# A decoder layer on one core: experts' rows from two factors, quantised tiles in pairs, maxima beside the norm's root

## What is computed

```python
x = x + attention(layernorm(x))                    # 16 heads, low-rank q and kv, rotary part
x = x + quantised_expert(layernorm(x), fside, ctx) # per batch
x = x + top2_of_8_experts(layernorm(x))            # silu(x w1) * (x w3) w2, weighted

def smooth_quant_linear(x, w):        # x [512, D], w [O, D]
    s = sqrt(max|x| per column / max|w| per column)
    xs, ws = x / s, w * s
    x_scale, w_scale = row maxima of |xs|, |ws|, each / 127
    return (round(xs / x_scale) @ round(ws / w_scale).T) * x_scale * w_scale.T

def quantised_expert(x, fside, ctx):
    gate, up = split(smooth_quant_linear(x, fside))
    return smooth_quant_linear(silu(gate) * up, ctx)
```

## Time and profile before

| | |
|---|---|
| median of 3 runs | 1187.24 us (1186.02 to 1187.73) |
| profiled execution | 1186.23 us, its span 1184.4 us |
| busy in the span | PE 990.1 (84%), DVE 968.2 (82%), ACT 670.5 (57%), POOL 291.5 (25%) |
| attention with its preparation | to about 868 us |
| last projections beside the first norm | 868 to 897 us |
| quantised layers | 897 to 1057 us |
| experts | 1057 to 1184.4 us |

### The profile page before, as it was taken

How to read it: one execution, slowest core, us unless ns; L and a number is a source line. 1 busy time by engine, 2 the same in 40 slices (tenths; PEclk the granted TensorE clock), 3 DMA queues, 4 the chain that set the end, 5 groups by cost and what they waited for, 6 DMA issues and landing times.

```text
span 1184.4 us, 18766 instructions
## 1 busy us (share of the span) xinstructions
PE 990.1 (84%) x6124; PEld 574.9 (49%) x6124; DVE 968.2 (82%) x2685; ACT 670.5 (57%) x1465; POOL 291.5 (25%) x508
## 2 busy tenths in 40 slices
PE   0456667999999999999999999999887565659997
PEld 0234444555555555555555555555445353435553
DVE  5757749989989888989989988888857888758886
ACT  1446557676666666667666666665504765743331
POOL 1036523232232222223223222221110222221110
PEclk9768679999999999999999999999988788769999
DMA  9300004333333336433325343345357130002323
GB/s 348 135 1 1 1 14 70 74 72 59 70 65 63 69 62 131 73 56 70 71 58 137 63 68 59 68 96 104 74 186 202 48 107 1 0 1 44 82 72 89
DMA packets 217328, 90.77 MB, mean 77 GB/s; under 512 B 191497, under 2 KB 202761, under 8 KB 216721
## 3 DMA queue, kind: packets, MB, share of 16 engines
q1 hardware_dynamic: 217232, 89.58, 32.7%
HBM read 36.06 MB, written 7.34 MB: 37 GB/s over the span
## 4 chain that ended last, share of the span: by engine, by line
PE 51%; DVE 31%; ACT 7%; issue 5%; POOL 3%; DMA 3%; SPq 0%; DVEq 0%; POOLq 0%; ACTq 0%
PE bank L1914 12%; PE bank L1864 8%; PE bank L1899 6%; PE bank L1812 3%; PE bank L1843 3%; DVE arena L774 3%; DVE arena L687 2%; PE bank L1882 2%; DVE arena L689 2%; PE bank L1886 2%; PE bank L1884 2%; PE bank L1885 2%; PE bank L1883 2%; DVE arena L1515 2%; DVE arena L1522 1%
## 5 line engine op out<-in xcount | busy, mean ns | idle before, releaser
L1204 ACT ACTIVATE arena<-bank,arena,scal 128x128 f32<-128x128 f32 (+3 forms) x256 | 157.7, 616 | 112.3 <-POOL arena L1045 111.2
L1914 PE MATMUL bank<-arena 128*128 128x512 f16 x768 | 179.2, 381 | 1.9 <-DVE arena L1548 1.9
L1522 DVE SCALAR_TENSOR_TENSOR arena<-arena 128x128 f16<-128x128 f32 (+3 forms) x256 | 142.2, 555 | 9.1
L1864 PE MATMUL bank<-arena 128*128 128x512 f16 x576 | 137.6, 385 | 0.0
L1045 POOL TENSOR_TENSOR arena<-arena,scal 128x1 f32<-128x1 f32 x256 | 51.2, 201 | 347.5 <-DVE arena L1498 345.8
L1515 DVE TENSOR_SCALAR arena<-arena 128x128 f16<-128x128 f32 (+3 forms) x256 | 125.4, 490 | 7.4 <-DVE arena L1507 0.8
L1498 DVE TENSOR_REDUCE arena<-bank 128x1 f32<-128x128 f32 (+3 forms) x256 | 123.7, 483 | 7.8 <-PE bank L1887 6.7
L1899 PE MATMUL bank<-arena 128*128 128x512 f16 (+3 forms) x768 | 117.6, 304 | 11.2 <-DMA arena<-arena 6.0
L1914 PEld LDWEIGHTS bank<-arena 128*128 128x128 f16 x768 | 73.1, 98 | 81.1 <-issue 4.7
L1899 PEld LDWEIGHTS bank<-arena 128*128 128x128 f16 x768 | 71.8, 99 | 62.7 <-issue 16.1
L1223 ACT ACTIVATE arena<-bank 32x512 f32<-32x512 f32 x128 | 75.2, 587 | 26.1 <-PE bank L1843 24.8
(11 more groups left out here) (200 smaller groups left out, 2053.5 us busy)
## 6 DMA issues: line engine op xcount, KB each, us to landing
arena<-in_L_attn_w_qb SPq DMA_DIRECT2D x1, 4608.0 KB, 21.6
arena<-arena SPq DMA_TRANSPOSE x272, 2.8
arena<-in_x SPq DMA_DIRECT2D x4, 1024.0 KB, 6.9
arena<-in_L_attn_w_o SPq DMA_DIRECT2D x1, 4096.0 KB, 31.9
arena<-in_fside_BxS2xS SPq DMA_DIRECT2D x4, 1024.0 KB, 7.3
arena<-in_L_ffn_w SPq DMA_DIRECT2D x8, 512.0 KB, 7.5
out<-arena SPq DMA_DIRECT2D x16, 256.0 KB, 2.3
arena<-in_x SPq DMA_DIRECT2D x12, 256.0 KB, 2.9
```

Of the source, the lines that this page charges most:

```text
L1204: act.activation(pf(k), banks[S_BANKS[G % 3]][:, 0:n], ACT.Exp, bias=NB[:, k:k + 1], scale=sc_exp, accum_out=SUM[:, k:k + 1]).then_inc(s_e ...
L1522: dve.scalar_tensor_tensor(out=ph_part(k, 1), in0=pf(k).rearrange("p (t c) -> p t c", c=P), scalar=R4[:, k:k + 1], in1=ph_part(k, 0), op0= ...
L1864: last = pe.matmul(banks[Q_BANK][:, :], wq(a, c, (i & 7) * 2 + h), ct(bp, b, c, 0, L), start=(k == 0), stop=(k == 3 * QC - 1))
L1914: last = pe.matmul(banks[Y_BANK][:, :], ot(gp, a, k, (q & 3) * P, P), wo(b, gp * GH + k), start=(k == 0 and n == 0), stop=(k == GH - 1 and ...
```

## The change

Three edits:

1. In the experts, GpSimd makes a second column, minus mean times inverse root (`mnr`), and ScalarE makes the normalised rows as x times the root plus that column. VectorE's `apply` goes. ScalarE's `apply(n + 2)` stands behind `front(n + 1)` and ahead of `silus(n + 1)`. Three waits keep the columns from being overwritten.
2. Two rounded tiles are transposed into the two halves of one bank, and ScalarE copies both with one instruction. TensorE waits for no copy within a matrix; the matrix's pair k waits for the rows' pair k.
3. `norm_batch` is cut in two. In the second round `norm_rows` stands inside `scales`, behind the four reductions of the matrix; in the first round it stays directly behind `norm_batch`.

```diff
@@ -328,7 +328,8 @@
         MH = take(E * FF, bf16)
         MHT = [take(E * FF, bf16) for _ in range(2)]
         ms = take(100)
-        m6, mmv, mcar, meps, mrs = ms[:, 0:6], ms[:, 6:8], ms[:, 8:9], ms[:, 9:10], ms[:, 10:11]
+        m6, mmv, mcar, meps, mrs, mnr = (
+            ms[:, 0:6], ms[:, 6:8], ms[:, 8:9], ms[:, 9:10], ms[:, 10:11], ms[:, 11:12])
         SCO, MX, IXF, IOTA, WV, WV2 = (ms[:, 16 + 8 * k:24 + 8 * k] for k in range(6))
         IX = ms[:, 64:72].bitcast(u32)
         DZ, EZ, DEN, P1, P2, mcar2 = (ms[:, 72 + k:73 + k] for k in range(6))
@@ -490,7 +491,11 @@
 
             def rstd_of(n):
                 pool.wait_ge(m_var, n + 1)
+                if n > 0:
+                    pool.wait_ge(m_norm, n)
                 pool.tensor_tensor(mrs, meps, half[:, 0:1], ALU.pow).then_inc(m_rstd, 1)
+                pool.wait_ge(m_rstd, 2 * n + 1)
+                pool.tensor_scalar(mnr, mmv[:, 0:1], mrs, -1.0, ALU.mult, ALU.mult).then_inc(m_rstd, 1)
 
             def second(n):
 
@@ -544,10 +549,10 @@
                 wid, li = LIN[l][0], layer_of(r, l, u)
                 c = wid // P
                 tr, te, dst = ((x_t, x_te, QXT), (w_t, w_te, QWT))[kind]
-                for t in range(TB):
-                    act.wait_ge(tr, li * TB + t + 1)
-                    act.activation(dst[u].rearrange("p (c q) -> p c q", c=DC)[:, 0:c, t * P:(t + 1) * P],
-                                   bankb[4 * u + t % 2][:, 0:wid].rearrange("p (c q) -> p c q", c=c),
+                for k in range(2):
+                    act.wait_ge(tr, li * TB + 2 * k + 2)
+                    act.activation(dst[u].rearrange("p (c t q) -> p t c q", c=DC, t=TB)[:, 2 * k:2 * k + 2, 0:c],
+                                   bankb[4 * u + k].rearrange("p (t c q) -> p t c q", t=2, c=DC)[:, :, 0:c],
                                    ACT.Copy).then_inc(te, 1)
 
             def output_scales(r, l, u):
@@ -579,6 +584,12 @@
             act.wait_ge(w2_in, 16)
             act.activation(W2B, W1S, ACT.Copy).then_inc(w_cast, 1)
 
+            def apply(n):
+                act.wait_ge(m_rstd, 2 * n + 2)
+                if n > 0:
+                    act.wait_ge(m_t, n)
+                act.activation(MXT, xall(n), ACT.Identity, bias=mnr, scale=mrs).then_inc(m_norm, 1)
+
             def front(n):
                 act.wait_ge(m_t, n + 1)
                 act.activation(XTB, banks[0][:, :], ACT.Copy).then_inc(m_tb, 1)
@@ -592,12 +603,17 @@
                     last = act.activation(MSG[n % 2][:, k * 512:(k + 1) * 512], banks[2 + k][:, :], ACT.Silu)
                 last.then_inc(m_silu, 1)
 
+            apply(0)
             front(0)
+            apply(1)
             silus(0)
             front(1)
+            apply(2)
             for n in range(1, NT - 1):
                 silus(n)
                 front(n + 1)
+                if n + 2 < NT:
+                    apply(n + 2)
             silus(NT - 1)
 
         def later_dve(dve, tail):
@@ -634,6 +650,10 @@
                 dve.wait_ge(q_agg, s + 1)
                 dve.tensor_scalar(qeps, qmv.rearrange("p (t a) -> p t a", a=2)[:, :, 1], 1e-5, None, ALU.add)\
                     .then_inc(q_var, 1)
+
+            def norm_rows(r, u):
+
+                s = r * 2 + u
                 dve.wait_ge(q_rstd, s + 1)
                 for t in range(TB):
                     dve.tensor_scalar(NX[u][:, t * D:(t + 1) * D], xall(batch_of(r, u) * TB + t),
@@ -648,6 +668,8 @@
                 link = chain(c_own, li, 4)
                 am = AM[u]
                 for t in range(2 * TB):
+                    if t == TB and l == 0 and r > 0:
+                        norm_rows(r, u)
                     a = (TB + t if t < TB else t - TB) * 4
                     dve.wait_ge(c_t, li * 2 * TB + t + 1)
                     dve.tensor_reduce(AMT[u][:, a:a + c], banks[4 * u + t % 4][:, 0:wid].rearrange("p (c q) -> p c q", c=c),
@@ -704,7 +726,7 @@
                     X = XB[batch_of(r, u)]
                     dve.tensor_tensor(X, X, HF[u], ALU.add).then_inc(x2_made, 1)
 
-            tail(norm_stats, norm_batch, scales, quantise)
+            tail(norm_stats, norm_batch, norm_rows, scales, quantise)
             for h in HALVES:
                 r, l, u = h
                 prev = preceding(h)
@@ -729,19 +751,14 @@
                 dve.bn_stats(m6, xall(n)).then_inc(m_stat, 1)
                 dve.wait_ge(m_stat, n + 1)
                 dve.memset(mcar, 0.0)
+                if n > 0:
+                    dve.wait_ge(m_rstd, 2 * n)
                 dve.bn_aggr(mmv, m6).then_inc(m_agg, 1)
                 dve.wait_ge(m_agg, n + 1)
                 dve.tensor_scalar(meps, mmv[:, 1:2], 1e-5, None, ALU.add).then_inc(m_var, 1)
 
-            def apply(n):
-                dve.wait_ge(m_rstd, n + 1)
-                if not (n == 0):
-                    dve.wait_ge(m_t, n)
-                dve.tensor_scalar(MXT, xall(n), mmv[:, 0:1], mrs, ALU.subtract, ALU.mult).then_inc(m_norm, 1)
-
             def norm(n):
                 stats(n)
-                apply(n)
 
             def route(n):
 
@@ -793,7 +810,6 @@
                 gate(n)
                 stats(n + 2)
                 add_out(n - 1)
-                apply(n + 2)
                 route(n + 1)
             gate(NT - 2)
             add_out(NT - 3)
@@ -832,15 +848,13 @@
 
             def quantised_t(r, l, u, kind):
                 wid, li = LIN[l][0], layer_of(r, l, u)
-                made, done, te = ((qx_r, x_t, x_te), (qw_r, w_t, w_te))[kind]
+                made, done = ((qx_r, x_t), (qw_r, w_t))[kind]
                 for t in range(TB):
                     pe.wait_ge(made, li * TB + t + 1)
-                    if t >= 2:
-                        pe.wait_ge(te, li * TB + t - 1)
-                    elif kind == 1:
-                        pe.wait_ge(x_te, li * TB + TB)
+                    if kind == 1 and t % 2 == 0:
+                        pe.wait_ge(x_te, li * 2 + t // 2 + 1)
                     for q in range(wid // P):
-                        last = pe.transpose(bankb[4 * u + t % 2][:, q * P:(q + 1) * P],
+                        last = pe.transpose(bankb[4 * u + t // 2][:, t % 2 * D + q * P:t % 2 * D + (q + 1) * P],
                                             rounded_rows(l, u, kind)[:, t * D + q * P:t * D + (q + 1) * P], identb[:, :])
                     last.then_inc(done, 1)
 
@@ -854,7 +868,7 @@
 
             def layer(r, l, u):
                 c, li = LIN[l][0] // P, layer_of(r, l, u)
-                pe.wait_ge(w_te, li * TB + TB)
+                pe.wait_ge(w_te, li * 2 + 2)
                 for t in range(TB):
                     if t == 3:
                         pe.wait_ge(wsb_made, li + 1)
@@ -1740,17 +1754,19 @@
             out_lo(2 * NPAIR - 2)
             out_lo(2 * NPAIR - 1)
 
-            def tail(norm_stats, norm_batch, scales, quantise):
+            def tail(norm_stats, norm_batch, norm_rows, scales, quantise):
                 add_y(NPAIR - 5)
                 norm_stats(0, 0, 0)
                 norm_stats(0, 0, 1)
                 norm_batch(0, 0)
+                norm_rows(0, 0)
                 add_y(NPAIR - 4)
                 scales(0, 0, 0)
                 add_y(NPAIR - 3)
                 norm_stats(0, 1, 0)
                 norm_stats(0, 1, 1)
                 norm_batch(0, 1)
+                norm_rows(0, 1)
                 add_y(NPAIR - 2)
                 quantise(0, 0, 0, 0)
                 add_y(NPAIR - 1)
```

## The result

| | before | after |
|---|---|---|
| median | 1186.63 us (4 runs, 1184.40 to 1187.73) | 1169.85 us (4 runs, 1168.90 to 1171.18) |
| ratio | | 0.9862, 95% interval 0.9843 to 0.9880 |
| profiled execution, its span | 1186.23 us, 1184.4 us | 1171.18 us, 1169.4 us |

The medians differ by 16.8 us, the spans of the two profiled executions by 15.0; the profiled execution of after is the slowest of its four. "Product" is the first quantising product of a half layer's rows (L687 before, L709 after; in the first half layer that of the matrix), `stats(0)` the first statistics of the experts.

The account below looks back on a forecast made before the run. VectorE was taken as the chain in the quantised layers and experts' loop. Gains 3.7 + 2.2 + 1.2 + 1.9 + 7.5 = 16.5 us gave 1170.7 us; own range 1167 to 1173, high end 1176 with rivals.

Parts of the forecast that it names:

- (a): Quantised layers: the wait moves to ScalarE and half of the 9.0 us is lost; 1175.2 us; chance 0.10.
- (e): Whole change: bank halves still held back, rows come no earlier; within 2 us of before; chance 0.03.
- Rows on ScalarE: Experts' loop: VectorE loses `apply`, 0.61 us a block, period 7.06 to 6.45; 7.9 over 13 blocks, 7.5 net.
- (b): Experts' loop: ScalarE's queue sets the period at 6.75 us; 1174.6 us; chance 0.08.
- (c): Experts' loop: TensorE, held by the turned rows, sets the period at 6.67 us; 1173.5 us; chance 0.06.
- (b2): Experts' loop: ScalarE's dearer pass lengthens the period, 7.06 + 0.23 us; 1181.2 us; chance 0.02.
- (d): Experts' loop: ScalarE changes its function table twice in every block; slower, 1199 us; chance 0.03.
- The start: Start of the experts' loop: the longer way through GpSimd and ScalarE costs about 0.4 us, once.
- The pairs: Quantised layers: TensorE no longer held by copies; 3.7 us in the first half layer, 2.2 and 1.2 elsewhere.
- Edges: Before each of four second-kind half layers: VectorE's wait for TensorE shrinks by 0.54 us each, 2.2 together.
- the last half layer: End of the quantised layers: TensorE's 2.43 us wait for a copy goes; 1.2 us, between 0 and 2.43.
- The maxima: Second round's norm, two places: four matrix reductions cover the wait for GpSimd's root; 0.95 us each, 1.9.

Follow-up runs that it names:

- the large copy: Changed kernel plus an unused ScalarE copy of 864 columns directly behind each `apply` in the experts' loop: 1174.68 us, ratio 0.9898.
- a shorter sum: Changed kernel with the experts' residual sum made for 128 of 512 columns only: 1169.47 us, ratio 0.9854.
- edit 1 alone: Kernel before with only the experts' normalised rows moved to ScalarE, quantised layers as before: 1180.84 us, ratio 0.9960.
- the reversed one: Changed kernel with ScalarE's order turned in the experts' loop, `silus(n)` ahead of `apply(n+1)`: 1176.06 us, ratio 0.9912.
- edit 3 alone: Kernel before with only the matrix's maxima put ahead of the normalised rows in the second round: 1182.02 us, ratio 0.9963.
- four copies: Changed kernel, two tiles to a bank and TensorE free, but each tile copied by its own instruction, four instead of two per matrix: 1170.04 us, ratio 0.9855.
- edit 2 alone: Kernel before with only the quantised tiles put two to a bank and copied in pairs: 1178.31 us, ratio 0.9932.
- TensorE's order: Changed kernel with the next half layer's row transposes and `spread` ahead of the transposes back, before second-kind layers: 1167.31 us, ratio 0.9840.

## Why the prediction was right, point by point

**Bound and mechanism.** Right in both stages: the gain came where VectorE waited or worked, and the waits went that the sum had named. Each edit alone moves its own stretches by what it moves in the whole change. With that, (a) and (e) fell: of the 9.0 us for the quantised layers nothing was lost to ScalarE, 10.0 came.

**Rows on ScalarE**, predicted 7.9 for the loop: 7.69. The step of 0.61 was 0.61 in the twelve undisturbed blocks (7.06 to 6.45); in the mean it is 0.592 (7.057 to 6.465), for the one block of 6.65. The way through ScalarE was forecast to end 6.1 after the gate and ended at 5.98 (1079.87 less 1073.89): the product took 0.27 where I took 0.2, the pass 0.81 instead of 0.78, but the two silus 1.06 instead of 1.19, since they overlap. So 0.47 spare instead of 0.35, and rival (b) fell by measurement; a longer ScalarE is what brings it about (6.828 with the large copy). (Its own steps, 6.1 and six times 0.1, make 6.70 and not the 6.75 that it was priced with.) Rival (c) was near: 6.42 was forecast for TensorE, and that is what the gates that wait for it show with a shorter sum. The power behind GpSimd's product was not held in the steady blocks: it waits 0.16 for VectorE.

Rival (b2), a period of 7.29, fell as well: edit 1 alone has 6.499. The pass is dearer on ScalarE, 0.81 against 0.55, but it lies in time that ScalarE had to spare. The rule of the Trainium skill against the change, additions and products on VectorE ("ScalarE: Activation LUTs", Rules for kernel authors), has the direction of that price right and doesn't decide the period here. Rival (d) fell too: the last table load stands at 865.0 us. That agrees with the Trainium skill, which puts identity into every set ("ScalarE: Activation LUTs", Table sets).

**The start** cost 0.66 instead of 0.4. The step counted the longer way of one block's rows; the first gate waits 2.85 us for silus queued behind `apply(1)` as well. That this order is the price is shown by the reversed one, where the start takes 19.21 us.

**The end of the loop** was not in the sum, and gives back 2.08 us. From `gate(14)` to the end (after; the window over the last `down`, then in order of time):

```profile
1162.49:1165.03 2.54, 2.54 (x8) 0.77 (x8) 0.00 (x0) 0.00 (x0) 0.00 (x0) 0.72 0.28 108
```

```profile
1157.21 2.16 DVE L791 SCALAR_TENSOR_TENSOR arena<-bank,arena 128x128 bf16<-128x128 f32 x8 [0.49 <-PE bank L933]
...
1162.49 2.54 PE L942 MATMUL bank<-arena 128*128 128x512 bf16 x8 [3.65 <-DMA arena<-arena]
...
1165.08 0.69 DVE L798 TENSOR_TENSOR arena<-bank,arena 128x512 f32<-128x512 f32 x1 [5.11 <-PE bank L942]
```

Before, in the same views:

```profile
1179.29:1181.19 1.90, 1.90 (x8) 0.69 (x8) 0.00 (x0) 0.00 (x0) 0.00 (x0) 1.00 0.37 142
```

```profile
1174.00 2.16 DVE L774 SCALAR_TENSOR_TENSOR arena<-bank,arena 128x128 bf16<-128x128 f32 x8 [0.20 <-DMA arena<-arena]
...
1179.29 1.90 PE L928 MATMUL bank<-arena 128*128 128x512 bf16 x8 [3.50 <-DMA arena<-arena]
1181.22 0.69 DVE L781 TENSOR_TENSOR arena<-bank,arena 128x512 f32<-128x512 f32 x1 [4.46 <-PE bank L928]
```

The last gate comes 5.72 after `gate(14)`, before 5.43: with VectorE's step shortened, `up` is late, 0.29. The last `down` has a granted clock of 0.72 instead of 1.00, so a part of it runs at 1.2 GHz, after 3.65 us idle instead of 3.50, and takes 2.54 instead of 1.90: 0.66 to the last sum. From that sum to the end it is 4.32 instead of 3.18, 1.14. That is the last store, which lands 3.2 us after its issue instead of 2.0. In the view of the DMA, after and then before (queue: packets, MB, share; issue: count, KB, us to landing):

```profile
q8 instruction: 1, 0.02, 2.4%
...
out<-arena SPq DMA_DIRECT2D x1, 256.0 KB, 3.2
```

```profile
out<-arena SPq DMA_DIRECT2D x1, 256.0 KB, 2.0
```

While the store is under way, the queue that the profile calls instruction moves one packet of 16 KB. Only one other kernel has that, the one with ScalarE's order turned, and its last store takes 2.7; in the ten without it takes 2.0. The slow turns of the hidden rows go with the same queue: of the 192 turns in the twelve traces, the 154 with no such packet between issue and landing took 3.04 to 3.12 us, the 6 with one of 8 KB 3.44 to 3.49, and the 32 with one of 16 KB 3.03 to 4.86, 27 of them 3.4 or more. The last such turn of edit 1 alone, and then the one ahead of it:

```profile
q8 instruction: 1, 0.02, 1.4%
...
arena<-arena SPq DMA_TRANSPOSE x1, 4.6
```

```profile
arena<-arena SPq DMA_TRANSPOSE x1, 3.1
```

The kernels without edit 1 end in 15.83 to 16.33, those with it in 17.6 to 19.6. In five of the latter the last gate waits for such a slow turn (4.5 to 4.9 us), in four for `up`, and it comes 5.7 to 7.2 after `gate(14)`. Their last `down` takes 2.3 to 3.6; but in the kernels with edit 2 or edit 3 alone it takes 2.4 as well, so the fall of the clock is not of edit 1 alone. Of the 2.08 us only the 0.29 of the late gate is shown to follow from the edit. Why a packet meets just that turn in five of the nine kernels with the edit and in none of the other three, and why the clock falls, are open.

**The pairs**, 7.1 predicted, 7.48 measured. First half layer 3.82 against 3.7: the 0.1 for ScalarE's rounding was not lost, since GpSimd's root of the ratios lasts longer (to 909.26 us, the rounding to 908.99). Edges 2.14 against 2.2, but 0.37 to 0.82 apiece. The hole itself behaved as the step says, 0.57 to 0.59 at each for the 0.54 taken. At 6 to 7, the edge of the earlier trace rows, VectorE's wait for the `spread` shrinks as well, from 1.05 to 0.80, which is the upper bound's case. At 2 to 3 and 3 to 4 the four reductions behind the hole take 0.19 and 0.18 longer. That the sum came out is partly luck, and so is the last half layer, 1.52 where the middle of 0 to 2.43 was taken. The 0.16 a pair that ScalarE gains, noted beside TensorE's freedom and not in the sum, are worth nothing that shows, as four copies tell.

**The maxima**: mis-sized, 1.9 against 2.55, and above the bound of 1.15 each. Two steps failed. The last tile was not late: the row transposes took 2.03 us for four tiles, the faster pace. And the bracket of 1.13 understates what the wait cost: from the variance's last instruction to the next it was 1.31 (987.32 to 988.63), now 0.08 (981.40 to 981.48), so 1.23, since the instruction that isn't held starts before the one ahead has ended. Before:

```profile
987.32 0.17 DVE L635 TENSOR_SCALAR arena<-arena 128x4 f32<-128x4 f32 x1
```

**The sum.** By spans 15.0 was gained of 16.5: quantised layers 1.0 better, loop and start 0.5 worse, end 2.1 worse. By medians it was 16.8. The 1.8 between the two is no gain: the profiled execution of before lies 0.4 below the median of its four runs, that of after 1.3 above. The forecast of 1170.7 is 0.9 above the median and 0.5 below the profiled execution. That is closer than its terms: the errors cancel, and that they do is luck. The low end, called the sum of the better ends, took the edges and the last half layer at their middle; with their upper bounds of 3.4 and 2.43 that sum is 19.8 and not 17.4.

## What to carry to other kernels

Price a removed wait from start to start of the engine's instructions, not by the idle time in the bracket, and take it where the next engine's queue stands: the gain of two tiles a bank was that TensorE's queue ran past the copies, not that there were fewer of them. An operation can go to a slower engine if that engine's way from release to use ends ahead of its reader; count it in order of time, and then ask which engine is next (here TensorE, 0.03 us behind, with GpSimd's queue close by). Count the first and the last block of a loop by themselves, and look at the same stretch in kernels without the edit before you put its loss down to it.

## What the runs showed of the hardware that I had not expected

- A `spread` of 16 fp32 matmuls takes 2.05 us in after, at a granted clock of 1.00 (2.4 GHz). In the second norm of three other kernels (edit 2 alone, the short sum, TensorE's order) it takes 3.51, 3.62 and 3.51 at 0.56, 0.53 and 0.56: most of it runs at 1.2 GHz. VectorE then waits 2.0 to 2.2 us instead of 1.25. TensorE had been idle for 2.31, 2.20 and 2.35 us ahead of these, for 2.37 ahead of the quick one, so the idle time just ahead doesn't decide it.
- The turn of the hidden rows lands after 3.04 to 3.12 us unless a packet of the profile's instruction queue falls into it; with one of 16 KB it takes up to 4.86, and the last store 3.2 instead of 2.0. With the shorter period a slow turn can hold a block (0.36 us with edit 1 alone; one of 4.02 in after held none).
- The attention part, the same in all kernels, hands over its first product anywhere from 887.7 to 891.8 us. That is a third of a per cent, more than most of these edits' terms.
